# The last token group of a mixture of experts is routed between the first three expert steps

## The reference

```python
x = _layernorm(x + _L0_attn_ref(x, ...))
probs = softmax(x @ Wg)                      # 4096 x 8
weights, indices = top_k(probs, 2)
for e in range(8):
    y = gelu(x @ W1[e] + b1[e]) @ W2[e] + b2[e]
    out = out + y * cw[:, e:e + 1]           # cw: the two weights of a token, else 0
x = _layernorm(x + out)
```

## Time and profile before

| what | value |
|---|---|
| timed runs, median of 3 (lowest to highest) | 372.06 us (370.76 to 372.7) |
| span of the profiled execution, first to last instruction | 385.0 us |
| time of the profiled execution itself | not given beside its span |
| busy: PE, DVE, ACT, POOL | 275.6, 278.8, 233.1, 226.1 us |
| chunks | to about 141 us |
| steps | about 141 to 344 us |
| last send-back issued, results gathered and normed | 349 us, to the end |

### The profile page before, as it was taken

One profiled execution on the slowest core, in us unless ns is written; L12 is line 12 of the kernel. 1 busy time (PEld: TensorE's weight loads), 2 busy tenths in 40 slices (PEclk: granted clock), 3 DMA queues, 4 the chain that ended last, 5 costly groups with the idle time before them and its releaser, 6 DMA issues.

```text
span 385.0 us, 5368 instructions
## 1 busy us (share of the span) xinstructions
PE 275.6 (72%) x1329; PEld 225.6 (59%) x1329; DVE 278.8 (72%) x791; ACT 233.1 (61%) x498; POOL 226.1 (59%) x281
## 2 busy tenths in 40 slices
PE   1467998699867739339643039999999999962940
PEld 1234776377535429239533029999999999941410
DVE  2999889999984978409931027999999999930680
ACT  2406665577753756508731037999999999950461
POOL 4888156638867767710677724666666766671460
PEclk9999999789979968958986558999999999995885
DMA  3633203101101122120222213222222222115732
GB/s 103 197 95 115 78 1 109 56 0 49 43 28 48 43 69 64 42 56 22 58 88 99 95 63 104 84 83 86 82 85 81 68 84 83 61 43 207 282 103 82
DMA packets 27189, 31.19 MB, mean 81 GB/s; under 512 B 4632, under 2 KB 22560, under 8 KB 27160
## 3 DMA queue, kind: packets, MB, share of 16 engines
q1 hardware_dynamic: 22328, 20.89, 18.0%
q0 software_dynamic: 4832, 9.97, 7.7%
HBM read 16.99 MB, written 13.86 MB: 80 GB/s over the span
## 4 chain that ended last, share of the span: by engine, by line
DVE 41%; issue 20%; PE 15%; POOL 9%; DMA 5%; ACT 4%; DVEq 1%; another core or an unknown queue 1%; SPq 1%; ACTq 0%; POOLq 0%
DVE h_l L928 8%; DVE wuse L891 7%; POOL slots_d L448 5%; DVE h_h L924 4%; PE bank L1028 3%; PE bank L1030 3%; PE bank L1029 3%; DVE work L693 2%; DVE h_l L697 2%; POOL results_d L454 2%; PE bank L1170 2%; PE bank L1178 1%; ACT fw L616 1%; DVE xt_l L914 1%; DMA late<-slots_d 1%
## 5 line engine op out<-in xcount | busy, mean ns | idle before, releaser
L454 POOL DMA_INDIRECT results_d<-work,dest x87 | 88.7, 1019 | 54.6 <-ACT work L590 34.1
L448 POOL DMA_INDIRECT slots_d<-rows,slot_i x64 | 66.6, 1040 | 38.6 <-DVE rows L830 19.4
L574 ACT ACTIVATE h<-bank,buse 128x384 f32<-128x384 f32 x116 | 67.8, 584 | 32.8 <-issue 21.5
L928 DVE TENSOR_TENSOR h_l<-h,h_h 128x384 fp32r<-128x384 f32 x116 | 64.5, 556 | 27.4 <-ACT h_h L579 23.6
L1028 PE MATMUL bank<-h_h,wuse 128*128 128x384 f32 (+1 forms) x148 | 60.5, 409 | 3.9 <-DVE h_l L697 1.6
L1028 PE MATMUL bank<-xt_h,wuse 128*128 128x384 f32 x116 | 42.2, 364 | 26.1 <-issue 20.2
L1029 PE MATMUL bank<-h_l,wuse 128*128 128x384 f32 (+1 forms) x148 | 53.3, 360 | 0.0
L1030 PE MATMUL bank<-h_h,wuse 128*128 128x384 f32 (+1 forms) x148 | 53.2, 360 | 0.0
L520 ACT ACTIVATE h<-bank 128x512 f32<-128x512 f32 x32 | 19.0, 595 | 38.3 <-DVE h_l L697 18.8
L891 DVE CAST wuse<-fw 128x1024 fp32r x58 | 40.0, 691 | 1.4 <-issue 1.4
L1029 PE MATMUL bank<-xt_l,wuse 128*128 128x384 f32 x116 | 40.8, 352 | 0.0
(11 more groups left out here) (213 smaller groups left out, 610.4 us busy)
## 6 DMA issues: line engine op xcount, KB each, us to landing
late<-slots_d SPq DMA_DIRECT2D x29, 195.0 KB
late<-in_L_ffn_W_dram SPq DMA_DIRECT2D x16, 256.0 KB, 2.8
work<-in_L_attn_x3d_dram SPq DMA_DIRECT2D x8, 256.0 KB, 3.3
rows<-results_d SPq DMA_DIRECT2D x4, 512.0 KB, 5.1
work<-results_d SPq DMA_DIRECT2D x4, 512.0 KB, 8.5
out_dram<-fw SPq DMA_DIRECT2D x8, 256.0 KB, 2.3
slots_d<-zeros SPq DMA_DIRECT2D x9, 195.0 KB, 4.1
results_d<-work,dest POOLq DMA_INDIRECT x87
```

What stands on the lines that cost most here:

```text
L448: pool.indirect_dma_start(out=slots_d, out_offset=bass.IndirectOffsetOnAxis(ap=slot_i[:, k, i:i + 1], axis=0), in_=rows[:, k, i, :], in_of ...
L454: pool.indirect_dma_start(out=results_d, out_offset=bass.IndirectOffsetOnAxis(ap=dest[:, SQ * g + q:SQ * g + q + 1], axis=0), in_=yo[:, g ...
L574: act.activation(h32[:, b % 2, 0:SLOTS], H_PS[b % 2][:, 0:SLOTS], ACT.Gelu, bias=buse[:, k, b:b + 1]).then_inc(sm["gelu_b"], 1)
L928: dve.tensor_tensor(ht_l[b], h32[:, b % 2, 0:SLOTS], ht_h[b].bitcast(F32), ALU.subtract).then_inc(sm["hbl_ready"], 1)
```

## The change

`walk` is given the step with which the second phase starts, `FRESH` = 3, and treats it apart. Steps 1 and 2 no longer prepare step 3: step 1 leaves out its transposes, step 2 its first hidden blocks. Ahead of step 3 every engine finishes step 2, then calls `resume`, then does step 3 without a predecessor. `resume` holds what is left of the last routing (ScalarE: the exp; VectorE: weights and tiles) and then the start of step 3 and the transposes of step 4. The rest of the last routing moves up by a cut: the hits ahead of step 0, the ranks on TensorE ahead of step 1, exponents, ranks, tails and slots ahead of step 2. GpSimd scatters 4 DMAs of group 2, does the norm of chunk 7, and scatters the other 12. SP zeroes the tails ahead of the loads of steps 3 to 8, not ahead of those of step 9 on. The diff, cut to its core (on VectorE the weight casts of a step keep their place by conditions on g alone):

```diff
@@ sync
             for n in range(PHASES):
+                if n == 1:
+                    zero_tails()
                 if n == PHASES - 1:
-                    zero_tails()
                     sp.wait_ge(sm["prefilled"], 16)
@@ gpsimd
-            def dispatch(g, half):
+            def dispatch(g, a, b):
...
-                for i in range(GT * g + QT * half, GT * g + QT * (half + 1)):
+                for i in range(GT * g + a, GT * g + b):
...
-            for c in range(NCH + 2):
+            for c in range(NCH + 1):
...
-                if c >= GC + 2:
-                    dispatch((c - GC - 2) // GC, (c - GC - 2) % GC)
-
-            for half in range(GC):
-                dispatch(NG - 1, half)
+                if GC + 2 <= c < NCH:
+                    half = (c - GC - 2) % GC
+                    dispatch((c - GC - 2) // GC, QT * half, QT * (half + 1))
+
+            dispatch(NG - 2, 0, 2)
+            norm(NCH - 1)
+            dispatch(NG - 2, 2, GT)
+            dispatch(NG - 1, 0, GT)
@@ scalar
+            def resume():
+
+                second_exp()
+                x_high(FRESH, FRESH % 2)
+
-            walk(act, MT, step, {ROUTE3: lambda: act.wait_ge(sm["rt_ready"], NCH),
-                                 ROUTE3 + 1: lambda: rows_of(NCH - 1), ROUTE3 + 3: second_exp,
+            walk(MT, FRESH, step, resume,
+                                {1: lambda: act.wait_ge(sm["rt_ready"], NCH),
+                                 2: lambda: rows_of(NCH - 1),
@@ vector
             route_choice(NG - 1, 1)
+            route_hits(NG - 1)
 
             def last_stats():
                 stats(NCH - 1)
                 aggregate(NCH - 1)
-                route_hits(NG - 1)
 
             def last_ranks():
                 route_exponents(NG - 1)
                 route_ranks(NG - 1)
                 route_tails()
-
-            def last_weights():
+                route_slots(NG - 1)
+
+            def resume():
+
                 route_weights(NG - 1)
                 route_tiles(PHASES - 1)
                 dve.wait_ge(sm["route_ready"], PHASES)
+                x_low(FRESH, FRESH % 2)
+                meta(FRESH, FRESH % 2)
 
-            walk(dve, MT, step, {ROUTE3: last_stats, ROUTE3 + 1: last_ranks,
-                                 ROUTE3 + 2: lambda: route_slots(NG - 1), ROUTE3 + 3: last_weights})
+            walk(MT, FRESH, step, resume, {1: last_stats, 2: last_ranks})
@@ tensor
+            def begin(g, k):
+
+                pe.wait_ge(sm["w1use_ready"], g + 1)
+                pe.wait_ge(sm["xb_lo"], g + 1)
+                hidden(g, k, 0)
+                hidden(g, k, 1)
...
-            def after_last_rows():
-                pe.wait_ge(sm["row0_ready"], NCH)
+            def last_ranks():
+                pe.wait_ge(sm["lg_sb"], NCH)
                 ranks(NG - 1)
 
-            walk(pe, MT, step, {ROUTE3 + 1: after_last_rows})
+            def resume():
+                xt(FRESH, FRESH % 2)
+                begin(FRESH, FRESH % 2)
+                xt(FRESH + 1, (FRESH + 1) % 2)
+
+            walk(MT, FRESH, step, resume,
+                 {1: last_ranks, 2: lambda: pe.wait_ge(sm["row0_ready"], NCH)})
@@ walk
-def walk(eng, M, step, cuts):
+def walk(M, fresh, step, resume, cuts):
...
+    for g in range(M + 1):
         if g in cuts:
             cuts[g]()
-        step(g, g % 2, g < M, g >= 1, g + 1 < M, g + 2 < M, None)
-
-    for g in range(M + 1):
-        one(g)
+        if g == fresh:
+            step(g, g % 2, False, True, False, False)
+            resume()
+            step(g, g % 2, True, False, g + 1 < M, g + 2 < M)
+        else:
+            step(g, g % 2, g < M, g >= 1, g + 1 < M and g + 1 != fresh, g + 2 < M and g + 2 != fresh and g + 1 != fresh)
```

More of the change, by code:

```diff
@@ L49 @@
 GC = 2
-ROUTE3 = 1
 PIECES = (0, 6, 10, 13, 16)
@@ L80, in build @@
     NSL = MT * SLOTS
+    FRESH = begins[1]
     CAP = T + SLOTS
@@ L439, in norm @@
                 pool.tensor_tensor(nmr[:], nmean[:], rstd[:, QT * c:QT * (c + 1)], ALU.mult).then_inc(sm["nmr_ready"], 1)
-            def dispatch(g, half):
-                if half == 0:
+            def dispatch(g, a, b):
+                if a == 0:
                     pool.wait_ge(sm["routed"], g + 1)
                     pool.wait_ge(sm["row1_ready"], GC * (g + 1))
-                for i in range(GT * g + QT * half, GT * g + QT * (half + 1)):
+                for i in range(GT * g + a, GT * g + b):
                     for k in range(2):
@@ L562, in evacuate, with step @@
                                bias=buse[:, k, HB:HB + 1]).then_inc(sm["yt_ready"], 1)
-            def step(g, k, now, prev, nxt, far, nth):
+            def step(g, k, now, prev, nxt, far):
                 if prev and not now:
@@ L928, in step @@
                         dve.tensor_tensor(ht_l[b], h32[:, b % 2, 0:SLOTS], ht_h[b].bitcast(F32), ALU.subtract).then_inc(sm["hbl_ready"], 1)
-                        if b == 0 and far:
+                        if b == 0 and g + 2 < MT:
                             held.append(expert_of(g + 2))
@@ L932, in step @@
                             x_low(g + 1, 1 - k)
+                        if b == 1 and g + 1 < MT:
                             weights2(g + 1, 1 - k, held[g + 1])
+                        if b == 1 and nxt:
                             meta(g + 1, 1 - k)
-                        if b == 3 and far:
+                        if b == 3 and g + 2 < MT:
                             weights1(g + 2, k, held[g + 2])
@@ L1136, in step @@
                         if b == 2 and nxt:
[L1138 to L1141, removed]
+                            begin(g + 1, 1 - k)
                         if b == 3 and far:
@@ L1152, in _ @@
             xt(0, 0)
[L1153 to L1156, removed]
+            begin(0, 0)
             xt(1, 1)
             r_transposed(NCH - 1)
-            def after_last_rows():
-                pe.wait_ge(sm["row0_ready"], NCH)
+            def last_ranks():
+                pe.wait_ge(sm["lg_sb"], NCH)
                 ranks(NG - 1)
-            walk(pe, MT, step, {ROUTE3 + 1: after_last_rows})
+            def resume():
[4 more added lines that the diff above has]
+                 {1: last_ranks, 2: lambda: pe.wait_ge(sm["row0_ready"], NCH)})
             def x1_sum(c):
@@ L1178, in _ @@
                 mm(SUM_PS[c % len(SUM_PS)][:, :].rearrange("p (q d) -> p q d", q=QT), ident[:], y01(c)[:, 0], start=False, stop=True).then_inc(sm["f_sum"], 1)
-def walk(eng, M, step, cuts):
-    def one(g):
+def walk(M, fresh, step, resume, cuts):
+    for g in range(M + 1):
         if g in cuts:
             cuts[g]()
-        step(g, g % 2, g < M, g >= 1, g + 1 < M, g + 2 < M, None)
-    for g in range(M + 1):
-        one(g)
+        if g == fresh:
[4 more added lines that the diff above has]
+            step(g, g % 2, g < M, g >= 1, g + 1 < M and g + 1 != fresh, g + 2 < M and g + 2 != fresh and g + 1 != fresh)
 _INS = ["L0_attn_x3d", "L0_attn_nu_log", "L0_attn_theta_log", "L0_attn_B_re", "L0_attn_B_im", "L0_attn_C_re",
```

## The result

| | before | after |
|---|---|---|
| timed runs, median (lowest to highest) | 371.91 us (370.76 to 372.7), 4 runs | 359.51 us (357.89 to 361.84), 4 runs |
| ratio to before, 95% interval | | 0.9664 [0.9612, 0.9716] |
| span of the profiled execution | 385.0 us | 355.8 us |
| busy DVE, POOL | 278.8, 226.1 us | 278.3, 242.3 us |

Each timed run also gives its span: those of after are 355.8 to 359.7, some 2.1 us under the times. So next to nothing lies around the span, and before's timed runs, by the same 2.1, have spans of some 370, not the 356.6 that the prediction rebuilt.

What follows compares the result with a forecast made beforehand. The prediction took the last routing to bound the kernel: TensorE's wait for step 3's load, two routing cuts, group 3's late scatter. Send-backs ending at 314.0 instead of 320.4 gave 6.4 us, 372.06 - 6.4 = 365.7 us; range 360.0 to 370.5.

Steps and rivals of the forecast that it cites:

- the 356.6 that the prediction rebuilt: Timed span of the kernel before, rebuilt without the slow stretch: send-backs ending at 320.4, plus 36.2 to the span's end.
- By GpSimd's queue they begin at 205.83 and take 87 x 1.317: Kernel before: the send-backs on GpSimd, 1.317 us each, end at 320.4, later than the 319.3 by the steps.
- crawl: Slow stretch in before's profiled record, 191.71 to 243.72: four expert steps take 52 us, eight tail zeroings 28.49.
- The steps' 314.0: Changed kernel: send-backs end at 314.0 by the steps, b0(9) = 208.95 plus 105.06; GpSimd's queue alone would end at 306.8.
- Which leaves 15.4 of the 372.06 for what lies around it: Around the profiled span: 15.4 us of before's median left over beside the rebuilt 356.6, set against 9 to 15 around a kernel.
- The wait at step 9: Kernel before: step 9's transposes wait 3.15 us for their load behind group 3's scatter; in the changed kernel no wait.
- b0(3) to b0(5): First gelu on ScalarE of step 3 to that of step 5: 14.78 us before, near 10.5 forecast after.
- the 0.84 of the restart: At step 3, started afresh: 0.84 us over a plain step, which the forecast said may fall away.
- More than that: Rival: half of the 15.4 around the span is slow stretch, shed by zeroing the tails early; 358.0 us, chance 0.13.
- Nothing to win at step 9: Rival: steps 5 to 8 run slower than 4.851, only the 2.17 at b0(5) is left; 369.9 us, chance 0.14.
- the tails hold up step 3: Rival: tail zeroings on SP delay step 3's load, some 15 us at 28.49 for eight; 380.4 us, chance 0.09.
- VectorE holds the scatter back: Rival: seven DMAs of group 2 each wait for a whole weight cast, the twelfth 4.0 later; 369.7 us, chance 0.06.

Runs made afterwards that it cites:

- the second record: The kernel before, unchanged, run and profiled once more: 372.21 us, span 370.0.

## Why the prediction was wrong

**Direction right, size wrong, from one term.** The failed step is "By GpSimd's queue they begin at 205.83 and take 87 x 1.317". The 1.317 was read from three send-backs that began with a wait of 1.23 for a result, late in a record whose crawl had let the queue catch up, as if it were the pitch of a full queue. The wait itself is not in the 1.317, but it sets where in a step the three DMAs fall. Two wide casts of VectorE in that record, beside the first and the third of them:

```profile
317.50 0.68 DVE L891 CAST wuse<-fw 128x1024 fp32r x1
...
320.24 0.68 DVE L891 CAST wuse<-fw 128x1024 fp32r x1
```

The casts begin 0.11 and 0.26 into their DMAs, which end soon behind them and are 1.03 and 1.06 long, not the 1.65 of a DMA that a cast meets 0.83 in. Back to back the send-backs take 1.450 in before and 1.495 in after. With these, before's queue ends at 205.83 + 87 x 1.450 = 332.0, where 320.4 stood (the second record: 332.93 + 0.96), and after's at 192.2 + 87 x 1.495 = 322.3, where "would end 306.8" stood (measured 320.4 + 2.44 = 322.8). The steps' 314.0 then no longer end last. That sum gives 9.7 us; the interval of the ratio gives 10.6 to 14.4. So some 2.7 of the 12.4 are not in it. Reaching step 0 sooner would make up more than that in the two records, 3.6, but the nine records of the kernel after and its variants reach that point at 142.3 to 145.6, the three of before and its variant at 144.7 to 147.1. Whether the change moves it stays open.

**"Which leaves 15.4 of the 372.06 for what lies around it" failed with it.** Most of it was the missing queue: 332.0 - 320.4 = 11.6 of send-backs, not a launch. About 2.1 lies around the span. So the weighing of the Trainium skill (Runtime: NRT & Kernel Launch, The ~15µs preamble/postamble breakdown) had no object: by these runs neither 15 nor 9 us stand beside the span.

**The wait at step 9** was mis-sized, 3.15 for a loss of 5.6 in the second record and 5.4 with fewer send-backs. It counted for nothing in the whole kernel, since before's end hung on the queue.

**What held**, from step 0 on: the norm's wait (6 to 7 forecast, 6.49), 28 DMAs without a pause, group 3's scatter beginning 26.4 behind step 0 (26.67), step 3's transposes 30.7 behind (31.07), the first gelu of step 9 64.2 behind (63.62), the weights and the tiles' end there in time. b0(3) to b0(5) took 9.59 for 10.5: the 0.84 of the restart didn't show.

**The rivals.** *More than that*, 358.0, came near the time by a mechanism that isn't there: the timed runs' spans have no room for a crawl. *Nothing to win at step 9* and *the tails hold up step 3* fell by the rows, 9.00 us for eight tails with 5.8 to spare. *VectorE holds the scatter back* had the mechanism and looked in the wrong place: it was priced on seven scatter DMAs of group 2 and not on the 87 send-backs. The seven followed each other at (162.58 - 152.44)/7 = 1.45, where 1.38 was forecast and the rival had 1.95, so the twelfth begins 0.5 later behind the first than forecast, not 4.0. Of the 87, the mean DMA takes 1188 ns beside wide casts and 985 without. There the rule of the Trainium skill (SBUF — State Buffer, SBUF: two separate sides), that such a copy keeps GpSimd from writing a DMA's descriptors, agrees with the rows: the ends of cast and DMA lie 0.12 apart in fourteen send-backs. The 1.38 was read as the size of the effect beside a busy VectorE; beside the steps it is 1.45 to 1.50.

## What to carry to other kernels

A queue's pitch is read where the queue is full. Where an instruction waited for its data a moment before, the producer also sets what the next ones run beside: here the casts held three such DMAs to 1.317 each, and those of a full queue to 1.45 to 1.50. Whether the queue would keep up alone has to be reckoned with the durations beside the work that will run then. Before an idle stretch on a path is priced, ask which engine has no idle time from there to the end: in the second record of before, GpSimd's "issue" of 0.30 ahead of every send-back names the bound. The first record hid it: there the queue caught up during the crawl, and from 232.56 on GpSimd waited for a result 22 times, 34.1 us in all. The 19.4 us in which GpSimd stood before group 3 were worth more than any wait of the steps.

## What the runs showed that was not expected

An indirect DMA on GpSimd that is 0.83 us old when a wide cast of VectorE begins (1024 columns, 0.69 us) ends 0.12 us after the cast, 1.65 us long and not 0.96. Two casts of 512 columns in place of one gave the whole kernel 6.8 us by the ratios, 5.6 by the medians, though the steps became 0.13 us longer. And VectorE waits in turn: with the halves its `h_h` cast takes up to 0.59 us and not 0.36, ending 0.16 after the DMA that was under way.

Queue and steps can fall into step: from 193.69 to 247.13 the send-backs of after come in rounds of three, mostly 1.64, 1.09 and 1.16 long, and eleven such rounds take 53.44 us, 4.86 each, as long as a step. The queue, which alone at 1.26 would need 3.78 for three, gains nothing on the steps in that stretch.

A single record can hold a stretch for which the timed runs have no room: the crawl of the first record of before, with one wait of 18.82 us and tails of 28.49 for eight, is in none of the later records.
